# Last two layer normalisations of a transformer tower: power on GpSimd, residual on TensorE, finer store groups

## What is computed

```
h = relu(x @ W1m[b].T + b1m[b]);  out = h @ W2m[b].T + b2m[b]
res = x + out
ffn = (res - mean(res)) * rsqrt(var(res) + 1e-5) * lng + lnb
h   = x + ffn
out = (h - mean(h)) / sqrt(var(h) + 1e-5)
```

## Time and profile before

| | |
|---|---|
| median of 3 runs | 255.11 us |
| the runs | 242.66, 260.1, 255.11 us |
| the profiled execution's own time | 245.0 us |
| its span, first to last instruction | 243.1 us |
| mean granted TensorE clock in it | 0.858 of full speed |
| busy: PE, PEld, DVE, ACT, POOL | 185.2, 146.7, 150.8, 103.0, 47.7 us |

### The profile page before, as it was taken

How to read it: one execution, slowest core, us unless ns; L and a number is a source line. 1 busy time by engine, 2 the same in 40 slices (tenths; PEclk the granted TensorE clock), 3 DMA queues, 4 the chain that set the end, 5 groups by cost and what they waited for, 6 DMA issues and landing times.

```text
span 243.1 us, 8170 instructions
## 1 busy us (share of the span) xinstructions
PE 185.2 (76%) x3611; PEld 146.7 (60%) x3611; DVE 150.8 (62%) x335; ACT 103.0 (42%) x185; POOL 47.7 (20%) x64
## 2 busy tenths in 40 slices
PE   0799989985955936878687999999999998881000
PEld 0799975543833635755287878888888977771000
DVE  1444296563899998899844354656665344458970
ACT  2000046463451333323633336677766233425782
POOL 0000016200567776000000000000007000006660
PEclk9999999997987775589955559999999999999555
DMA  7999984225553200000001101121300000000012
GB/s 222 393 392 386 372 125 103 76 76 127 124 131 89 55 3 4 5 0 4 0 3 47 53 3 50 53 73 32 86 16 3 3 3 3 5 3 1 18 52 67
DMA packets 11107, 19.82 MB, mean 82 GB/s; under 512 B 2030, under 2 KB 6830, under 8 KB 10432
## 3 DMA queue, kind: packets, MB, share of 16 engines
q1 hardware_dynamic: 11072, 19.30, 27.4%
HBM read 15.20 MB, written 0.82 MB: 66 GB/s over the span
## 4 chain that ended last, share of the span: by engine, by line
PE 39%; DVE 25%; SPq 21%; issue 6%; ACT 4%; POOL 2%; DMA 1%; ACTq 0%; POOLq 0%
PE PS L1074 17%; SPq L350 8%; PE PS L1096 7%; SPq L322 5%; DVE arena L302 5%; PE PS L1086 4%; SPq L345 3%; DVE sm L700 2%; DVE mx L688 2%; ACT t L607 2%; PE PS L1123 2%; DVE t L646 2%; DVE st L848 2%; PE PS L1119 2%; SPq L363 2%
## 5 line engine op out<-in xcount | busy, mean ns | idle before, releaser
L302 DVE COPY arena<-PS 128x1024 f32<-128x1024 f32 x32 | 39.2, 1225 | 44.6 <-PE PS L1074 44.6
L1074 PE MATMUL PS<-gates,wrow 18*128 18x128 f32 x1024 | 42.8, 314 | 5.0 <-DVE arena L302 4.1
L301 ACT ACTIVATE arena<-PS 128x1024 f32<-128x1024 f32 x32 | 32.8, 1025 | 32.3 <-PE PS L1074 32.3
L1074 PEld LDWEIGHTS PS<-gates,wrow 18*128 18x128 f32 x1024 | 37.1, 216 | 11.1 <-DVE arena L302 7.9
L895 PE MATMUL PS<-hid,arena 128*128 128x128 f32 (+1 forms) x208 | 28.0, 297 | 7.5 <-DVE hid L625 7.5
L895 PEld LDWEIGHTS PS<-hid,arena 128*128 128x128 f32 (+1 forms) x208 | 26.4, 206 | 8.9 <-issue 8.6
L954 PE MATMUL PS<-hid,arena 128*32 128x200 f32 x256 | 16.7, 415 | 8.7 <-DMA hid<-arena 8.5
L456 ACT ACTIVATE sd<-mv,epsc 128x2 f32<-128x2 f32 (+1 forms) x15 | 4.3, 293 | 37.2 <-DVE mv L636 37.2
L1096 PE MATMUL PS<-arena,t 128*32 128x128 f32 x512 | 19.9, 303 | 0.0
L625 DVE TENSOR_REDUCE hid<-hid 128x256 f32<-128x1280 f32 x4 | 9.4, 2358 | 15.7 <-DMA hid<-conv_filter 15.7
L954 PEld LDWEIGHTS PS<-hid,arena 128*32 128x32 f32 x256 | 9.2, 131 | 15.3 <-DMA hid<-arena 8.0
(11 more groups left out here) (104 smaller groups left out, 282.4 us busy)
## 6 DMA issues: line engine op xcount, KB each, us to landing
arena<-windows SPq DMA_DIRECT2D x24, 256.0 KB, 7.9
wrow<-ffn_weights SPq DMA_DIRECT2D x32, 128.0 KB
hid<-arena SPq DMA_DIRECT2D x32, 100.0 KB, 2.2
hid<-conv_filter SPq DMA_DIRECT2D x4, 640.0 KB, 7.3
cst<-consts SPq DMA_DIRECT2D x1, 1098.0 KB, 16.5
wrow<-ffn_weights SPq DMA_DIRECT2D x64, 8.0 KB
out<-t SPq DMA_DIRECT2D x16, 50.0 KB
arena<-windows SPq DMA_DIRECT2D x4, 64.0 KB, 8.1
```

What stands on the lines that cost most here:

```text
L301: return eng.activation(dst, PS[:, b:b + 2, :], ACT.Copy)
L302: return eng.tensor_copy(dst, PS[:, b:b + 2, :])
L1074: mm = pe.matmul(PS[:, merge_bank(n) + r, :].rearrange("p (b k j) -> p k b j", k=4, j=NJ)[:, k], wrow[32 * r:32 * r + KR, w], gates[32 * r ...
```

## The change

Five things, all in or around the last two normalisations:

1. TensorE adds the residual. `apply2` gets, for c = 0, 1, 2, additional matmuls that add x (feature-major, `t3`) times a permuted identity `identp` into bank 4 + q: images b = c, c + 3, ... of the quarter, so 6, 5 and 5 of them, 16 in a quarter. GpSimd makes `identp` (128 x 128) once, when the constants have arrived and ahead of its `kb` instructions. VectorE's `residual` is gone.
2. `bn_stats` of L = 2 reads PSUM bank 4 + q, and ScalarE's normalisation of L = 2 reads PSUM too and undoes the interleaving as it writes `t4`.
3. ScalarE's square root and VectorE's reciprocal are gone. GpSimd's `rstd` adds 1e-5 to the variances (one instruction, 4 or 2 columns) and raises them to the power -0.5 (`tensor_tensor` with `pow` against a tile of -0.5), with a wait between. VectorE's `last_shift` then waits for GpSimd.
4. The order. L = 2 goes by quarters, one after the other, then L = 3 by groups of 4, 4, 4, 2, 2 tiles. VectorE does statistics and shift of a group back to back. GpSimd has an order written out, `rstd` and gain/bias of pairs mixed.
5. Five store groups of the same sizes. In the last, SP issues two of the four DMAs and ScalarE the other two.

```diff
...
 NPS = NG // 2
-LAG = 3
+GROUPS = [(0, 4), (4, 4), (8, 4), (12, 2), (14, 2)]
 NU8 = NG // 2
...
+        mvl = sb("mvl", 2 * 2 * NG)
+        sdl = sb("sdl", 2 * NG)
+        rsl = sb("rsl", 2 * NG)
+        nms = sb("nms", 2 * NG)
+        identp = sb("identp", P)
+        halves = sb("halves", 4)
         st = [sb(f"st{i}", NG * 6) for i in range(4)]
...
         ffn_done = sem("ffn_done")
-        res_ready = sem("res_ready")
+        identp_ready = sem("identp_ready")
         x2b_ready = sem("x2b_ready")
         last_sd_done = sem("last_sd_done")
+        halves_set = sem("halves_set")
         last_rstd_done = sem("last_rstd_done")
...
+        def last_cols(L, a, n):
+            k = a + (NG if L == 3 else 0)
+            return slice(k, k + n)
...
                 eng.wait_ge(applied, cc - 1 - NC)
+        def store_rows(eng, i, a, n):
+            out_v = out_d.rearrange("(g i q) d -> i q g d", i=4, q=NS)
+            src = t5[32 * i:32 * i + NS, a * TM:(a + n) * TM].rearrange("p (g d) -> p g d", d=D)
+            eng.dma_start(out_v[i][:, a:a + n, :], src).then_inc(stored, 16)
...
+            for g, (a, n) in enumerate(GROUPS):
+                sp.wait_ge(norm_done[3], a + n)
+                for i in range(4 if g < len(GROUPS) - 1 else 2):
+                    store_rows(sp, i, a, n)
+            sp.wait_ge(stored, 16 * 4 * len(GROUPS))
...
             pool.memset(t3[:, NTOK:TP], 0.0).then_inc(pads_set, 1)
+            pool.memset(halves[:, :], -0.5).then_inc(halves_set, 1)
             pool.memset(rowc[:, :], 0.0).then_inc(rowc_zeroed, 1)
             pool.wait_ge(cst_loaded, 16)
+            pool.tensor_copy(identp[:, :].rearrange("p (s j) -> p s j", j=NJ), ident.rearrange("p (j s) -> p s j", j=NJ)).then_inc(identp_ready, 1)
...
             pool.wait_ge(x2b_ready, 1)
-            for s in range(NPS):
+            pool.wait_ge(halves_set, 1)
+            def rstd(L, a, n, done):
+                pool.wait_ge(aggr_done[L], a + n)
+                v = mvl[:, :].rearrange("p (t x) -> p t x", x=2)[:, last_cols(L, a, n), 1]
+                k = last_cols(L, a, n)
+                pool.tensor_scalar(sdl[:, k], v, 1e-5, None, ALU.add).then_inc(last_sd_done, 1)
+                pool.wait_ge(last_sd_done, done)
+                pool.tensor_tensor(rsl[:, k], sdl[:, k], halves[:, 0:n], ALU.pow).then_inc(last_rstd_done, 1)
+            def affine(s):
                 pool.wait_ge(norm_done[2], 2 * (s + 1))
-                c = slice(s * ST, (s + 1) * ST)
+                c = slice(s * 2 * TM, (s + 1) * 2 * TM)
                 v = t4[:, c].rearrange("p (t d) -> p t d", d=D)
                 pool.tensor_tensor(t4[:, c], t4[:, c], t1[:, c], ALU.add).then_inc(aff_done, 1)
+            rstd(2, 0, 4, 1)
+            affine(0)
+            rstd(2, 4, 4, 2)
+            affine(1)
+            affine(2)
+            rstd(2, 8, 4, 3)
+            affine(3)
+            rstd(2, 12, 4, 4)
+            affine(4)
+            rstd(3, 0, 4, 5)
+            affine(5)
+            rstd(3, 4, 4, 6)
+            affine(6)
+            affine(7)
+            rstd(3, 8, 4, 7)
+            rstd(3, 12, 2, 8)
+            rstd(3, 14, 2, 9)
...
+            def last_norm(L, i, done):
+                act.wait_ge(shift_done, done)
+                c, k = slice(i * TM, (i + 1) * TM), last_cols(L, i, 1)
+                if L == 2:
+                    src = PS[:, 4 + i // 4, (i % 4) * TM:(i % 4 + 1) * TM].rearrange("p (s j) -> p j s", j=NJ)
+                    to = t4[:, c].rearrange("p (j s) -> p j s", j=NJ)
+                else:
+                    src, to = t4[:, c], t5[:, c]
+                act.activation(to, src, ACT.Identity, bias=nms[:, k], scale=rsl[:, k]).then_inc(norm_done[L], 1)
+            for i in range(0, 4):
+                last_norm(2, i, 1)
...
+            for i in range(14, 16):
+                last_norm(3, i, 9)
+            act.wait_ge(norm_done[3], 16)
+            for i in range(2, 4):
+                store_rows(act, i, 14, 2)
...
+            def last_stats(L, a, n):
+                for i in range(a, a + n):
+                    src = PS[:, 4 + i // 4, (i % 4) * TM:(i % 4 + 1) * TM] if L == 2 else t4[:, i * TM:(i + 1) * TM]
+                    dve.bn_stats(st[L][:, 6 * i:6 * i + 6], src).then_inc(stats_done[L], 1)
+                for i in range(a, a + n):
+                    dve.wait_ge(stats_done[L], i + 1)
+                    k = i + (NG if L == 3 else 0)
+                    dve.bn_aggr(mvl[:, 2 * k:2 * k + 2], st[L][:, 6 * i:6 * i + 6]).then_inc(aggr_done[L], 1)
+            def last_shift(L, a, n, done):
+                dve.wait_ge(last_rstd_done, done)
+                k = last_cols(L, a, n)
+                m = mvl[:, :].rearrange("p (t x) -> p t x", x=2)[:, k, 0]
+                dve.scalar_tensor_tensor(out=nms[:, k], in0=m, scalar=-1.0, in1=rsl[:, k],
+                                         op0=ALU.mult, op1=ALU.mult).then_inc(shift_done, 1)
+            for q in range(NQ):
                 dve.wait_ge(ffn_done, q + 1)
...
+                last_stats(2, 4 * q, 4)
+                last_shift(2, 4 * q, 4, q + 1)
+            for g, (a, n) in enumerate(GROUPS):
+                dve.wait_ge(aff_done, (a + n) // 2)
+                last_stats(3, a, n)
+                last_shift(3, a, n, NQ + g + 1)
...
                     pe.wait_ge(gtok_done, 1)
+                    pe.wait_ge(identp_ready, 1)
                 if c == 0:
...
                                    start=False, stop=(c == NC - 1), skip_group_check=True)
+                if c < NC - 1:
+                    for b in range(c, QI, NC - 1):
+                        im = q * QI + b
+                        mm = pe.matmul(PS[32 * (b % 4):32 * (b % 4) + 32, 4 + q, (b // 4) * D:(b // 4 + 1) * D],
+                                       t3[:, im * NS:im * NS + 32], identp[:, :], start=False, stop=False, skip_group_check=True)
                 if c == NC - 1:
```

## The result

| | before | after |
|---|---|---|
| median, all executions | 248.88 us (4) | 254.18 us (4) |
| the executions | 242.37, 242.66, 255.11, 260.1 | 251.06, 254.07, 254.29, 254.86 |
| profiled execution, its span | 245.0, 243.1 | 254.86, 253.1 |
| ratio | | 1.039, 95% interval [1.031, 1.047] |

The change makes the kernel 3.9% slower. The time of 254.18 us lies in the predicted range of 246 to 266; the change of 1.8% that I forecast lies outside the interval. That the time came so near to the forecast of 256.5 is luck, as the part on the prediction shows.

The account below looks back on a forecast made before the run. Bounds: TensorE to 196.8 us, its merges alternating with VectorE's copies to 216, then a tail on VectorE and ScalarE. Residual +1.5, tail +3.7, stores -0.7 make +4.5 on a base of 252: 256.5 us, range 246 to 266.

Parts of the forecast that it names:

- the forecast: Whole kernel: power up to 0.46 us and shifts losing the race to GpSimd, 256.5 us; chance 0.32.
- a tail over 27 us: Chunk 3's first quarter to the last norm: the forecast is wrong if this takes under 23 or over 27 us.
- TensorE's residual: Second layer's chunks: six added matmuls a quarter cost chunk 0 +1.5 us; five each in chunks 1 and 2 cost nothing.
- Statistics, affine, norms, lock: Tail: four tiles' statistics 1.24 us, an affine (gain/bias pair) 1.52, two norms 0.87, a locked-out shift 0.73.
- The power, X: Tail, GpSimd's power before each of nine shifts: taken as 0.4 us, kept between 0.2 and 1.28.
- The intervals one by one: Tail, counted from shift to shift: 2.01, 3.38, 3.95, 2.66 three times, 3.77, 1.55 twice, 1.07; sum 25.26 against 21.60 us.
- Stores: After the last norm: two store issues on each of two queues, -0.7 us, bounds -0.9 and +0.5.
- The sum of +4.5: Whole kernel: residual 1.5, tail 3.7, stores -0.7 us, giving 245.0 to 249.5 in the profiled execution.
- The base of 252: Assumed time of the kernel before, between the mean of four executions (250.7 us) and their median (255.11).
- the power is dear: Tail, VectorE's nine waits behind GpSimd: 0.9 us per 0.1 of power; at 1.0, +9.9 and 262 us; chance 0.35.
- slower had 0.38 in all: Whole kernel: dear power 0.35 plus residual matmuls not hidden in chunks 1 and 2 (259 us) 0.03.
- The lock: Tail: shifts 2 to 6 lose the port to GpSimd and take 0.73 us; tail 25.3 with it, 23.8 without.

Follow-up runs that it names:

- 3, 5, 5, 3: Kernel before with the residual on TensorE, these counts of matmuls per quarter in chunks 0 to 3, old order and roots, five store groups; median 241.89 us, ratio 0.989.
- the eighteen that were run to test it: Kernel before with residual on TensorE and five store groups: twelve executions with 6, 5, 5 matmuls (240.84 to 245.11 us), six with 3, 5, 5, 3 (240.94 to 244.15).
- power alone: Kernel before, lag order and VectorE residual kept, with only the roots moved to GpSimd's addition and power; ratio 1.035.
- residual late: Kernel before with only the residual on TensorE, its matmuls in chunks 1, 2, 3 instead of 0, 1, 2; ratio 0.984 without the two long executions.
- residual late with stores: Kernel before with the residual on TensorE in chunks 1 to 3 and the five store groups; ratio 0.985.
- stores alone: Kernel before with only the five store groups, the last shared by SP and ScalarE; one execution, 245.57 us.

## Why the prediction came out as it did

The mechanism stood, one term was mis-sized. By the prediction's own sign, a tail over 27 us, the forecast was wrong. By its steps:

- **TensorE's residual:** +1.5 forecast, +1.9 measured (0.44 a round for 0.38). Chunks 1 and 2 hide theirs, as said.
- **Statistics, affine, norms, lock:** 1.24 forecast and 1.17 measured; shifts 2 to 6 took 0.68 (0.73 forecast), 1 and 7 to 9 took 0.16. With a multiplication in the power's place the tail was 23.0 us, where the count of the prediction with 0.2 gives 25.26 - 9 x 0.2 = 23.5.
- **The power, X:** taken as 0.4, "nearest to the square root plus a little for software". It is 1.04 with four columns and 0.71 with two. Counted for all nine, the miss is 7 x 0.64 + 2 x 0.31 = 5.1 us, nearly all that the forecast lacks: 25.26 + 5.1 = 30.4, and the tail is 30.1. This is the step that failed. The row that I chose from was another engine's; no row of GpSimd bounded a power from above.
- **The intervals one by one:** with the measured power in the forecast's place they are 2.65, 4.02, 4.59, 3.30 three times, 4.41, 1.86 twice and 1.07. Measured: 2.76, 3.97, 4.48, 3.23, 3.21, 3.21, 4.30, 1.92, 1.93 and 1.07. So the sum isn't right by errors that cancel.
- **Stores:** -0.7 forecast, -1.0 measured. 0.3 of it is the last wait for the data, 2.1 against 2.4, which in the unchanged kernel is 2.0 to 2.4 by chance.
- **The time:** 256.5 forecast, 254.18 measured, and this nearness is luck. The sum of +4.5 was 5.5 too low against the two profiled spans. The base of 252 was too high for the changed kernel, since it averaged in the long executions, which that kernel doesn't show; the other 30 in 42 of the kernel before lie at 240.9 to 246.8.
- **Which case:** the rival "the power is dear" came true, at its own price: +9.9 for X = 1.0. The spans differ by 10.0, but that includes +1.6 of half clock and -0.96 ahead of the change; the terms that the rival names make 1.9 + 8.5 - 1.0 = 9.4. It had 0.35, the forecast 0.32; slower had 0.38 in all. Since the count multiplied the one unknown by nine, the likeliest single value of X deserved less weight than it got.
- **The lock:** it was there, but no run shows the 1.5 us that I gave it (25.3 against 23.8). With the power at 1.04 GpSimd's queue is the next bound right behind it, and lifting the lock by a wait gained nothing (30.49 against 30.08).

Where the parts stand, in tail times of the runs: 21.6 before; 18.4 with the residual on TensorE; 20.3 with the serial order as well; 30.1 with the roots on GpSimd. The residual gains in the tail (and costs 1.9 of it ahead of the tail), the order is a small loss, and the power is 9.8 us, more than the whole loss. Best of both: the residual as 3, 5, 5, 3, the old order and roots, five store groups. Its median is 241.89 us, against 244.4 for the twelve short executions of the kernel before on that chip, and the ratio 0.989 [0.983, 0.995]. That is a small gain, within 2%.

## The half clock in chunk 0

Of 42 timed executions of the kernel before, beside these experiments, 12 took 255 to 264 us; the other 30 took 240.9 to 246.8. Its long profile puts 9.0 of the 13.3 us lost in chunk 0 of the second layer and the rest in chunk 1. All kernels with residual matmuls in chunk 0 (the changed one and six experiments), 44 executions, have none; if executions are independent, at 12 in 42 that would come by chance less than once in a million, and the eighteen that were run to test it would be clean with a chance of 0.2%. Kernels without them there (power alone, residual late, residual late with stores, stores alone) have 6 long ones in 15. In the changed kernel's profile the clock falls at the same place, at about 184 us, but is back after 4 us; short falls like it are in the profiles of two more kernels with them (stretch 36.8), in the second profile of before (34.98) and in that of the power alone (34.96). What TensorE did before the fall is the same in all: transposes and a bias round, after a pause of 0.16 us. It is the same in profiles without a fall too (183.28 of the kernel before), so it doesn't tell when the clock falls. What differs is what stands in chunk 0: bias and merge matmuls of 18 rows and image matmuls of 128 in all kernels, and in the changed one residual matmuls of 128 rows besides. Two more profiles point the same way: with the residual in chunks 1 to 3 the half clock ends in the first round that has residual matmuls (at about 207 us), without any it lasts to about 219. That the long fall doesn't come with them in chunk 0 is shown by the counts; why, and whether the rows or the number of matmuls matter, is open. So the change has a side that the ratio hides: it takes away the kernel's worst executions. Its mean of four (253.6) is 2.0% over the mean of those 42 (248.5, from other rounds), not 3.9%.

## What to carry to other kernels

An unknown price that a serial chain pays nine times must be priced from a row of the same engine, or the forecast belongs to the wide case. Before an instruction is moved to another engine, add up that engine's queue for the stretch: here 2.8 of every 3.2 us of GpSimd were then taken, and neither the lag order nor a wait that lifts the lock helped. Work that fits in TensorE's idle time, where it alternates with the copy of its result, was nearly free (0.02 us a round); about the same work in a stretch where TensorE is the bound cost its full length (0.44). And a forecast time that comes true can hold two errors that cancel: check the terms, not the total.

## Not expected of the hardware

- GpSimd's power takes 1.04 us for 128 x 4 and 0.71 for 128 x 2, so by an estimate from these two points 0.16 a column and 0.39 besides; a multiplication of the same shape takes 0.20.
- ScalarE's two DMA issues at the end take 0.94 us in the changed kernel and 0.86 to 0.87 in seven others, so 0.43 to 0.47 each, against some 0.35 on SP.
- A fully busy TensorE can be granted half its clock (1.2 GHz) in the same stretch of the same program for some 4 us or for some 34: the execution of 245.55 us and the one of 258.32 us of the kernel before. From 186 to 216 us of the latter it is busy in 30.00 of 30.00 us at 0.50.
